# A graph network layer with a dense mixer: another division of labour in the first layer normalisation

## The reference

```python
def reference(x, src, dst, edge_type, ...):        # x: 384 x 1024
    xn = layernorm(x)
    # attention over a graph: 16 heads, 384 nodes, 12288 edges
    q2 = (xn @ wq.T + bq) @ wiq.T + biq            # k2, v2 in the same way
    mask = -inf, then mask[src, dst] = softplus(edge_type_weights)[edge_type - 1]
    gnn = softmax(q2 k2 / 8 + mask) v2 @ wo.T + bo
    # mixer: features exp(-q^2/2), exp(-k^2/2), one coefficient a head
    mix = (sum(fq * fk) * v) @ Wo + bo
    x = x + gnn + mix
    # dense layer and one expert of eight, chosen from moments of the input
    z = layernorm(x)
    return x + z @ base_W.T + base_b + expert(z)
```

## Time and profile before

| | |
|---|---|
| median of 3 runs | 472.8 us (472.56 to 473.14) |
| profiled execution, its own time | 472.28 us |
| its span, first to last instruction | 470.5 us |
| PE, DVE busy | 462.7 us (98%), 341.7 us (73%) |
| ACT, POOL busy | 258.7 us (55%), 153.4 us (33%) |
| mean granted clock of PE | 0.998 |

### The profile page before, as it was taken

How to read it: one execution, slowest core, us unless ns; L and a number is a source line. 1 busy time by engine, 2 the same in 40 slices (tenths; PEclk the granted TensorE clock), 3 DMA queues, 4 the chain that set the end, 5 groups by cost and what they waited for, 6 DMA issues and landing times.

```text
span 470.5 us, 7320 instructions
## 1 busy us (share of the span) xinstructions
PE 462.7 (98%) x2521; PEld 429.9 (91%) x2521; DVE 341.7 (73%) x787; ACT 258.7 (55%) x423; POOL 153.4 (33%) x178
## 2 busy tenths in 40 slices
PE   7999999999999999999999999999999999999996
PEld 5999999999999888999999999999998888888885
DVE  6979876776636347688888888897875993586394
ACT  3724533333314244878979698897965362153270
POOL 4246667767777761001010202202044000050200
PEclk9999999999999999999999999999999999999999
DMA  8877776566544465477676747767669854210553
GB/s 247 324 235 213 233 213 168 180 181 184 155 131 159 129 206 197 156 236 262 198 226 205 240 154 228 246 211 232 195 210 364 276 214 135 89 45 1 169 236 134
DMA packets 39097, 91.92 MB, mean 195 GB/s; under 512 B 7458, under 2 KB 20354, under 8 KB 38932
## 3 DMA queue, kind: packets, MB, share of 16 engines
q1 hardware_dynamic: 33540, 83.02, 55.9%
q0 software_dynamic: 4864, 7.45, 4.7%
q10 hardware_dynamic: 656, 0.98, 0.6%
HBM read 77.96 MB, written 13.47 MB: 194 GB/s over the span
## 4 chain that ended last, share of the span: by engine, by line
PE 91%; DMA 2%; DVE 2%; ACT 2%; SPq 1%; issue 0%; DVEq 0%; ACTq 0%
PE PS L1327 34%; PE PS L1337 28%; PE PS L1332 17%; PE PS L1465 4%; PE PS L1453 2%; PE PS L1589 2%; PE PS L1395 2%; DMA U<-x 1%; PE PS L1315 1%; ACT U L684 1%; PE PS L1593 1%; DVE U L1303 1%; PE PS L1573 1%; DMA turn<-U 1%; DMA U<-turn 1%; ACT w_hi L561 0%
## 5 line engine op out<-in xcount | busy, mean ns | idle before, releaser
L936 DVE TENSOR_TENSOR w_lo<-raw,w_hi 128x1024 fp32r<-128x1024 f32 x86 | 104.3, 1225 | 45.8 <-ACT w_hi L561 45.7
L561 ACT ACTIVATE w_hi<-raw 128x1024 fp32r<-128x1024 f32 x87 | 91.0, 1054 | 72.8 <-PE PS L1337 46.0
L477 POOL DMA_INDIRECT table<-evalue,where x96 | 102.5, 1068 | 42.5 <-issue 26.0
L1332 PE MATMUL PS<-xT_hi,w_lo 128*128 128x384 f32 x320 | 61.9, 334 | 0.0
L1327 PE MATMUL PS<-xT_lo,w_hi 128*128 128x384 f32 x320 | 61.9, 334 | 0.0
L1327 PE MATMUL PS<-xT_hi,w_hi 128*128 128x384 f32 x320 | 61.9, 334 | 0.0
L1332 PEld LDWEIGHTS PS<-xT_hi,w_lo 128*128 128x128 f32 x320 | 56.0, 188 | 0.0
L1327 PEld LDWEIGHTS PS<-xT_lo,w_hi 128*128 128x128 f32 x320 | 56.0, 188 | 0.0
L1327 PEld LDWEIGHTS PS<-xT_hi,w_hi 128*128 128x128 f32 x320 | 56.0, 188 | 0.0
L1337 PE MATMUL PS<-w_hi,T_hi 128*128 128x512 f32 x144 | 40.1, 391 | 0.0
L1337 PE MATMUL PS<-w_hi,T_lo 128*128 128x512 f32 x144 | 39.9, 389 | 0.0
(11 more groups left out here) (247 smaller groups left out, 805.4 us busy)
## 6 DMA issues: line engine op xcount, KB each, us to landing
raw<-weights SPq DMA_DIRECT2D x84, 512.0 KB, 4.6
turn<-U SPq DMA_DIRECT2D x16, 576.0 KB, 3.8
U<-turn SPq DMA_DIRECT2D x64, 144.0 KB, 2.9
U<-key_dram SPq DMA_DIRECT2D x32, 192.0 KB, 4.2
mask<-weights SPq DMA_DIRECT2D x9, 512.0 KB, 5.1
table<-Q POOLq DMA_DIRECT2D x4, 576.0 KB
V<-conv SPq DMA_DIRECT2D x4, 512.0 KB, 5.1
U<-table POOLq DMA_DIRECT2D x3, 576.0 KB, 6.6
```

What stands on the lines that cost most here:

```text
L477: pool.indirect_dma_start(tables[g], bass.IndirectOffsetOnAxis(ap=where[:, k:k + 1], axis=0), evalue[:, k:k + 1], None, bounds_check=N * N ...
L561: act.activation(w_hi[slot][:], raw[slot][:], ACT.Copy).then_inc(hi_ready[slot], 1)
L936: dve.tensor_tensor(w_lo[slot][:], raw[slot][:], w_hi[slot][:].bitcast(F32), ALU.subtract).then_inc(lo_ready[slot], 1)
L1332: last = pe.matmul(o, wl, src[0][:, k, :], start=False, stop=(k == KB - 1))
```

## The change

The roots of the three tiles are taken by POOL as a power of -0.5, one tile at a time. POOL makes the identity for the transposes itself, splits the first weight block, and converts the edge keys before it writes the four tables. ACT scales tile 0 as before, but rounds the first weight ahead of the transposed tile, and copies both halves of tile 2; DVE scales tile 1 between the two halves of tile 2's statistics and copies tile 1's transpose. Tile 0 of `x` is loaded in quarters. The small constants come in one load; the broadcast load of the edge weights is gone. `FILL` is gone and `WARM` is 17.

```diff
-WARM = 21
-FILL = 4
+WARM = 17
 # SP
-            for t in range(NT):
+            for c in range(2):
+                q = slice(c * HALF, c * HALF + HALF // 2)
+                sp.dma_start(x_rows[:, 0, q], x[0:P, q]).then_inc(x_in[0][c], 16)
+            for t in range(1, NT):
                 sp.dma_start(x_rows[:, t, 0:HALF], x[t * P:(t + 1) * P, 0:HALF]).then_inc(x_in[t][0], 16)
-            sp.wait_ge(x_in[1][0], 16)
+            sp.wait_ge(x_in[0][1], 32)
             load_weights(*A_USES[0], weights[0])
-            sp.wait_ge(x_in[2][0], 16)
-            load_weights(*A_USES[1], weights[1])
-            sp.dma_start(cst[:, C_TRI:C_ALL], consts[:, C_TRI:C_ALL]).then_inc(cst_in, 16)
+            sp.dma_start(cst[:], consts).then_inc(cst_in, 16)
             sp.dma_start(erow_i, edge_rows).then_inc(edges_in, 16)
             sp.dma_start(ecol_i, edge_cols).then_inc(edges_in, 16)
-            sp.dma_start(bias[:], bias_cols).then_inc(const_in, 16)
-            sp.dma_start(disc_in[:], disc).then_inc(const_in, 16)
+            load_weights(*A_USES[1], weights[1])
             load_weights(*A_USES[2], weights[2])
...
-                sp.wait_ge(xt_done, NT)
+                sp.wait_ge(xt_turned, 2)
 # POOL
-            pool.dma_start(ew[:], edge_weights.partition_broadcast(P)).then_inc(ew_in, 16)
+            pool.memset(ident[:], 0.0).then_inc(ident_ready, 1)
...
+            pool.affine_select(ident[:], ident[:], [[-1, P]], ALU.not_equal, 1.0, base=0,
+                               channel_multiplier=1).then_inc(ident_ready, 1)
+            pool.memset(power[:], -0.5).then_inc(ident_ready, 1)
...
+            def first_root(t):
+
+                pool.wait_ge(spread_ready, 2 * t + 2)
+                pool.tensor_tensor(rstd[:, 2, t:t + 1], rstd[:, 0, t:t + 1], power[:], ALU.pow).then_inc(root_ready, 1)
+
+            first_root(0)
+            pool.wait_ge(root_ready, 1)
+            pool.tensor_scalar(rstd[:, 3, 0:1], mv[:, 0, 0:1], -1.0, rstd[:, 2, 0:1],
+                               ALU.mult, ALU.mult).then_inc(shift_ready, 1)
+            first_root(1)
+            first_root(2)
+
+            pool.wait_ge(xn_ready, 2)
+            split_lo(*A_USES[0])
+
+            pool.wait_ge(edges_in, 32)
+            pool.tensor_copy(erow, erow_i).then_inc(key_calc, 1)
+            pool.wait_ge(key_calc, 1)
+            pool.tensor_scalar(erow[:, 0:P], erow[:, 0:P], float(N), None, ALU.mult).then_inc(key_calc, 1)
+            pool.wait_ge(key_calc, 2)
+            pool.tensor_tensor(erow[:, 0:P], erow[:, 0:P], erow[:, P:2 * P], ALU.add).then_inc(key_calc, 1)
+            pool.wait_ge(key_calc, 3)
+            pool.dma_start(key_dram, erow[:, 0:P]).then_inc(key_out, 16)
+
             pool.wait_ge(blanked, 2)
-            pool.wait_ge(w_in[A_USES[0][0]], 16)
             for g in QUARTERS:      # the four tables
...
-            pool.wait_ge(key_calc, 1)
-            pool.dma_start(key_dram, erow[:, 0:P]).then_inc(key_out, 16)
 # ACT
+            for c in range(2):
+                q = slice(c * HALF + HALF // 2, (c + 1) * HALF)
+                act.dma_start(x_rows[:, 0, q], x[0:P, q]).then_inc(x_in[0][c], 16)
...
-            act.dma_start(cst[:, 0:C_TRI], consts[:, 0:C_TRI]).then_inc(id_in, 16)
-            act.activation(tiny[:, 24:25], w_lo[2][:, 0:1].bitcast(F32), ACT.Sqrt)
-            act.wait_ge(var_ready, 1)
-            act.activation(rstd[:, 1, 0:1], rstd[:, 0, 0:1], ACT.Sqrt).then_inc(rstd_guess, 1)
+            act.activation(tiny[:, 24:25], w_lo[2][:, 0:1].bitcast(F32), ACT.Exp)
             act.wait_ge(shift_ready, 1)
             act.activation(xn_rows[:, 0, :], x_rows[:, 0, :], ACT.Identity, scale=rstd[:, 2, 0:1],
                            bias=rstd[:, 3, 0:1]).then_inc(xn_first, 1)
-            act.wait_ge(var_ready, 2)
-            act.activation(rstd[:, 1, 1:NT], rstd[:, 0, 1:NT], ACT.Sqrt).then_inc(rstd_guess, 1)
-            for t in range(NT):
-
-                act.wait_ge(xt_turned, t + 1)
-                banks, r = turned(t)
-                ks = slice(0, 4 if t == 2 else KB)
-                act.activation(xT[0][:, ks, r], banks[:, ks, :], ACT.Copy).then_inc(xt_hi, 1)
-                if t == 0:
-                    split_hi(*A_USES[0])
+            split_hi(*A_USES[0])
+            act.wait_ge(xt_turned, 1)
+            banks, r = turned(0)
+            act.activation(xT[0][:, :, r], banks, ACT.Copy).then_inc(xt_hi, 1)
+            banks, r = turned(2)
+            act.wait_ge(xt_turned, 3)
+            act.activation(xT[0][:, 0:4, r], banks[:, 0:4, :], ACT.Copy).then_inc(xt_front, 1)
+            act.wait_ge(xt_turned, 4)
+            act.activation(xT[0][:, 4:KB, r], banks[:, 4:KB, :], ACT.Copy).then_inc(xt_rest, 1)
             split_hi(*A_USES[1])
+            split_hi(*A_USES[2])
 # DVE
+            def first_scaled(t):
+
+                dve.wait_ge(root_ready, t + 1)
                 dve.tensor_scalar(xn_rows[:, t, :], x_rows[:, t, :], mv[:, t, 0:1], rstd[:, 2, t:t + 1],
                                   ALU.subtract, ALU.mult).then_inc(xn_ready, 1)
+
+            for t in range(NT):
+                for c in range(2):
+                    if t == 2 and c:
+                        first_scaled(1)
+                    dve.wait_ge(x_in[t][c], 16 if t else 32)
+                    half_stats(t, c)
+                dve.wait_ge(norm_step, normed[0])
+                dve.bn_aggr(mv[:, t, :], stats[:, t, :, :].rearrange("p c s -> p (c s)")).then_inc(spread_ready, 1)
+                dve.wait_ge(spread_ready, 2 * t + 1)
+                dve.tensor_scalar(rstd[:, 0, t:t + 1], mv[:, t, 1:2], EPS, None, ALU.add).then_inc(spread_ready, 1)
+            first_scaled(2)
...
+            dve.wait_ge(xt_turned, 2)
+            mid, r1 = turned(1)
+            dve.tensor_copy(xT[0][:, :, r1], mid).then_inc(xt_mid, 1)
             for t in range(NT):      # xT[1] of each tile
-                dve.wait_ge(xt_hi, t + 1)
...
-            split_weights(*A_USES[0])
...
 # PE
-            for n in range(FILL):
-                pe.matmul(PS[:, 0, :], w_lo[2][:, 0:P], w_lo[2][:, P:P + HALF], start=True, stop=True)
...
+            pe.wait_ge(xt_mid, 1)
+            pe.wait_ge(xt_front, 1)
+            part_of(0, w_hi, 0, range(4), start=True)
             pe.wait_ge(xt_rest, 1)
-            first_part(slice(P, N), range(4, KB))
+            part_of(0, w_hi, 0, range(4, KB))
+            pe.wait_ge(lo_ready[A_SLOTS[0]], 2)
+            part_of(0, w_lo, 0, range(KB))
             pe.wait_ge(hi_ready[A_SLOTS[1]], 1)
-            whole_part(1, w_hi, 0, True, False)
+            part_of(1, w_hi, 0, range(KB), start=True)
             pe.wait_ge(xt_done, NT)
-            whole_part(0, w_hi, 1, False, False)
...
+            part_of(0, w_hi, 1, range(KB), stop=True).then_inc(w_used[A_SLOTS[0]], 1)
+            part_of(1, w_hi, 1, range(KB))
...
```

More of the change, by code:

```diff
@@ L106, with gps_layer @@
 LN_BANKS = ((6, 4, 2), (6, 4, 0))
-C_ID, C_TRI, C_ONES, C_EIDX, C_ONE, C_ALL = 0, 128, 256, 384, 392, 520
-def gps_layer(nc, x, out, weights, conv, down, upT, up_b, down_b, conv_b, disc, bias_cols,
-              rows, edge_weights, edge_rows, edge_cols, consts):
+C_TRI, C_ONES, C_EIDX, C_ONE, C_BIAS, C_EW, C_DISC = 0, 128, 256, 264, 392, 464, 468
+C_ALL = C_DISC + 2 * EXPERTS * KB
+def gps_layer(nc, x, out, weights, conv, down, upT, up_b, down_b, conv_b, rows, edge_rows, edge_cols, consts):
     with ExitStack() as ctx:
@@ L608, in _ @@
             act.activation(ew_t[:, 0:4], ew_t[:, 0:4], ACT.Ln, bias=1.0).then_inc(aprep, 1)
-            act.wait_ge(const_in, 32)
-            for a in range(2, DEPTH):
-                split_hi(*A_USES[a])
+            act.wait_ge(cst_in, 16)
             for a in range(FIRST):
@@ L870, in row_stats, with row_norm @@
                 dve.tensor_scalar(rstd[:, 0, t:t + 1], mv[:, t, 1:2], EPS, None, ALU.add).then_inc(var_ready, 1)
-            def row_norm(which, t, done):
-                v, y, z, m = (rstd[:, c, t:t + 1] for c in range(4))
-                dve.wait_ge(rstd_guess, t + 3)
+            def row_norm(t, done):
+                v, y, z = (rstd[:, c, t:t + 1] for c in range(3))
+                dve.wait_ge(rstd_guess, t + 1)
                 step(dve.reciprocal(y, y))
@@ L909, in first_roots @@
-            def first_roots(ts, guess):
-                c = slice(ts[0], ts[-1] + 1)
-                v, y, z = (rstd[:, n, c] for n in range(3))
-                dve.wait_ge(rstd_guess, guess)
-                step(dve.reciprocal(y, y))
-                step(dve.tensor_tensor(z, y, v, ALU.mult))
-                step(dve.scalar_tensor_tensor(out=z, in0=z, scalar=-0.5, in1=y, op0=ALU.mult, op1=ALU.mult))
-                step(dve.scalar_tensor_tensor(out=z, in0=z, scalar=1.5, in1=y, op0=ALU.add, op1=ALU.mult))
@@ L1384, in _, with part_of @@
             turn(2, xt_turned, halves=True)
-            def first_part(r, ks):
+            def part_of(a, wide, part, ks, start=False, stop=False):
```

(8 more changed lines are left out.)

133 lines of the change are left out of this document (45 added, 88 removed).

## The result

The changed kernel takes 476.06 us in the median (473.03 to 479.52, 18 runs), the kernel before 472.74 (471.92 to 474.02, 18 runs). The ratio is 1.0066, 95% interval [1.0052, 1.0081]: slower by 3.3 us where 1.6 faster was forecast.

A forecast was written before the change was run, and what follows sets the result against it. PE was taken as the bound, so only its start counts: first real work at 12.8 for 14.59 us gives 1.8, less 0.1 for handovers. 472.28 - 1.7 = 470.6 profiled, 471.1 as median; own range 470.5 to 471.7.

The forecast's parts named there:

- What bounds the kernel: Whole kernel: PE busy 462.7 of 470.5 us, so only its start counts; real work behaves as begun at 14.59.
- The load of x: Start: tile 2's first half lands at 7.64 us in place of 7.99; rival of no faster load, 471.8, chance 0.14.
- The broadcast's stall: Load of x: the edge-weight broadcast's packets hold the DMA engines; removing it brings x 0.72 us earlier.
- The packets of 1 KB: Load of x: tile 0's quarters halve the packets from 2 KB, costing 0.37 us more.
- The bound of 8.4 for tile 2: Load of x: latest landing of tile 2's first half, if the stall stays and small packets cost in full.
- From x to the scaled tile 2: DVE and POOL at the start: statistics, root and scaling end at 11.52 us, where before has 12.75.
- The rivals of the long power: POOL's roots: power of 1.02 us gives 472.1, chance 0.07; up to 2.40 gives 475.8, slower, chance 0.07.
- From there to PE's first product: Transposes and copies after scaling: PE starts at 12.8 in place of 14.59; gain 1.7 us after 0.1 off.
- Is it kept to the end?: Mask stream on POOL: scatters start at about 26 to 27 us, so none of the early gain is lost.
- If they stream at 402 GB/s: Table writes, 2.36 MB: scatters start at 26 to 27 us; at 13.5 us for the tables, about 30.3.
- The rival for it: Late mask: scatters at 30.3 to 31 lose 0.5 to 1.3 us of the gain, 472.0; chance 0.06.
- The clock: Rival at PE's start: idle time lowers its clock, costing 1.2 us, leaving gain 0.5, 472.3; chance 0.06.

The follow-up runs named there:

- both mends: Tile 0 of x in halves and the table writes issued between POOL's roots, against the changed kernel; 472.05 us, 0.9978 of the kernel before.
- tables in the gaps: POOL issues two table writes after root 1 and two after root 2, against the changed kernel; 474.38 us, 1.0034 of the kernel before.

## Why the prediction was wrong

**What bounds the kernel.** Right as far as it went: PE's first real work and the mask are what counts. The prediction read from the earlier trace rows that nothing later was worth naming. Nothing waits there in before, but the steps behind the mask have little slack, and that showed only when they became late.

**The load of x** is the step that failed first. It has two terms. The broadcast's stall was attributed rightly, but 0.72 us for it was too much: without it tile 2 is 0.2 earlier, and the median the same. The packets of 1 KB were put at 0.37 us, from the mean time of a packet of each size. DVE reads tile 1 7.84 - 5.85 = 2.0 us late in the changed kernel, and 2.9 in the kernel before with small packets alone. In the changed kernel the windows from 3.5 to 5.5 us have 197 to 225 GB/s:

```profile
3.50:4.00 0.50, 0.50 (x3) 0.40 (x2) 0.35 (x1) 0.49 (x2) 0.50 (x1) 1.00 1.00 197
...
4.50:5.00 0.50, 0.50 (x3) 0.40 (x2) 0.34 (x1) 0.00 (x0) 0.00 (x0) 1.00 0.61 213
```

In the first of these the packets themselves take far longer than the 52 to 81 ns of the estimate: 39 of one queue take 0.734 x 8 / 39 = 0.15 us each.

```profile
q1 hardware_dynamic: 39, 0.06, 73.4%
```

In the second the engines are busy for only 0.61 of the time. So neither the time of one packet nor that the engines go on without a pause can be taken from a window at 402 GB/s. That the quarters are the cause is shown by the run with halves. That it is their small packets more than their number is shown in the kernel before only, where the broadcast may add to it; what holds the engines is not shown. The bound of 8.4 for tile 2 left tile 1 where it was, and it was tile 1 that came late: at 7.84 it puts its whole statistics, 1.29, ahead of those of tile 2.

**From x to the scaled tile 2** was right. From the start of tile 1's scaling to the end of tile 2's the sum has 11.52 - 8.32 = 3.20 us, and by DVE's timeline after has 13.55 - 10.23 = 3.32 and the run with halves 11.49 - 8.18 = 3.31. The power was 0.55 to 0.57 in place of 0.4, and the first call took 0.57 like the others. The load of about 6 us at the first call to a freshly loaded kernel of the engine, of which the Trainium skill tells in GPSIMD Engine Reference, section 2.1, is not to be seen in this trace: the first root starts 0.17 after the epsilon behind 5.63 has ended, and no row ahead of it is that long. The rivals of the long power fell.

**From there to PE's first product.** With halves the first product starts at 12.98 and the third job at 21.40, against 12.8 and 21.2. The mechanism was right, and the gain at the start is 1.5 us of the predicted 1.7 once the packets are as they were. Weight 0 lands at 10.65, past the 10.1 that ACT was allowed; it did no harm, since tile 2 was later still.

**Is it kept to the end?** This is the step that failed second, and it has the larger share of the profiled execution. "If they stream at 402 GB/s" was chosen over "if the tables take the same 13.5 us as in before". They were issued at 18.63, not 16, and the last was in 31.72 - 18.63 = 13.1 us later. With halves it took 29.51 - 16.57 = 12.9, and in before with late tables 32.56 - 20.30 = 12.3. The reason given, that the weight loads would be out of the way, fails by the windows:

```profile
16.00:18.00 2.00, 2.00 (x13) 2.00 (x13) 2.00 (x3) 1.28 (x2) 1.50 (x5) 1.00 0.00 0
18.00:20.00 2.00, 2.00 (x14) 2.00 (x12) 1.74 (x6) 1.51 (x3) 2.00 (x3) 1.00 0.09 25
20.00:24.00 4.00, 4.00 (x25) 4.00 (x25) 3.54 (x13) 1.60 (x3) 1.67 (x3) 1.00 0.98 321
```

The DMAs stand almost idle from 16 to 20 us, and when the tables' packets start, the next weight blocks and the broadcasts of the keys start with them. The tables' 2.36 MB move as 1.14 MB from 20 to 24 us, where their queue (q0) has 0.87 of the engines, and 1.22 MB from 24 to 32, where SP's queue (q1) has more of them than that:

```profile
q1 hardware_dynamic: 682, 1.74, 59.8%
q0 software_dynamic: 311, 1.22, 40.8%
```

The late mask then costs more than its own lateness of the first scatter: 32.78 - 30.11 = 2.7 us there, 5.6 at the merge. POOL waits 11.4 us for earlier scatters in place of 9.5, which is 1.9 of the difference; what makes up the rest was not resolved. The rival for it had the right mechanism, at 472.0, with a scatter at 30.3 to 31 as its worst case.

**The clock** was given 0.06 and "longest 1.4 against 1.3". The mean clock is lower in 13 of 18 runs, but not in the profiled one, whose idle times at the start are 1.7 and 1.4. Where it falls in the 13 is inferred: in the traces of two relatives of this kernel it falls at the start, and with products of zeros put back it holds in 12 of 12 runs. With `x` on time it holds without them (12 of 12 runs with both mends, 8 of 10 with halves alone), and in the kernel before with quarters it is lower in 8 of 12 although that has its products of zeros, so the late `x` is behind it. The price of 1.2 us was read from products of 628 ns, but the granted clock was 1.00 there, and 628 is not twice 216, so that row says nothing of half speed. From the last transposes to the third job the changed kernel takes 23.47 - 13.61 = 9.9 us, with the tables in the gaps 23.85 - 12.94 = 10.9 and with weight 0 as in before 26.01 - 13.70 = 12.3: a fall costs 1.1 to 2.5.

**The later pairs** are in no step of the prediction. Their transfers land 5.0 to 5.6 us after issue in the changed kernel. A kernel whose start is 1.6 us early loses it there too, so they may be the reason why no kernel here is surely faster than before. What makes the transfers slow in one execution and not in another was not found. The direction of the change is explained by shown causes: the small packets, the late tables and the clock. How the 3.3 us of the median are split among them is not, since the three overlap: by the ratios, products of zeros win 1.8 us, earlier tables 1.5, halves 3.1, and the last two together 4.2. The order of the weight loads as in before wins 1.5 as well, in six runs, and that is not explained.

## What to carry to other kernels

- When a write that nothing needs at once is moved behind other work, ask what it was hidden under: the table writes beside the first weights held nothing up, and with them behind the key work the mask was complete 5.6 us later. Take the duration that they have in the trace, not one worked out from a peak rate.
- Cutting the first of several transfers into smaller packets brings that one forward and can delay those behind it by more, as here; look at when the last is in, not the first.
- Products of zeros that keep the clock are part of the schedule that they were tuned for. If what they bridge gets longer, they are needed more.

## What the runs showed of the hardware

- 1 KB packets for one tile of three, with the number of transfers and bytes unchanged, made DVE read the next tile 2.9 us later (8.72 against 5.85) and the kernel 2.8 us slower (ratio 1.0059), in the kernel before, with its broadcast.
- The granted clock of PE fell to 0.50 behind idle times of 0.87 and 1.44 us at the start (tables in the gaps), 4.0 us (quarters alone) and 4.57 us (late tables), and stayed at 1.00 in the profiled execution of the changed kernel behind 1.71 and 1.41.
- A GpSimd power on 128x1 takes 0.55 to 0.57 us, the first one too; a `tensor_scalar` on 128x1 takes 0.27.
- Four table writes of 576 KB take 12 to 13 us from issue to landing at each of three places in the schedule (issued at 16.6, 18.6 and 20.3 us), and 11.2 in the run with products of zeros back, about twice the 5.9 us that 2.36 MB would take at the 402 GB/s of the earlier trace rows.
- Issuing two of these costs POOL 1.9 us and issuing four 3.0; issuing four takes ScalarE 2.8, of which 1.2 lie beside its scaling of tile 0, and SyncE 3.8 to 4.1, in which no computing engine takes part.
